# Repeated rows ordered by tokens, blend's softmax by channels, weights quantised on GpSimd, tokens in halves ahead of the indices

## The reference, cut to what matters

```
y = x @ weight[id[b]].T + bias[id[b]]           # cond, one weight per sequence
q, k = silu(y Wq), silu(y Wk); rotate by cos/sin(theta * token); v = y Wv
o = (tril(q k^T) v) Wo * sigmoid(y G1 G2); x = x + layernorm(o)
ctx = causal_ema(x, tau_ctx)
g   = x * sigmoid([x, ctx] Wg + bg)
mod = 0.5 + sigmoid(gelu(x Wn1) Wn2)            # 8 factors for each token
traces[d] = causal_ema(g * mod[d], tau[d])      # 8 of them
temporal = sum_d traces[d] * softmax(blend, axis=0)[d]    # blend is 8 x 256
z = layernorm((gelu(x Wsoma) * sigmoid(temporal Wtemp)) Wout)
x = x + ffn(z)     # bit-linear: weights to -1, 0, 1 by their mean |w|; activations to 8 bits
```

## Time and profile before

| | before |
|---|---|
| median of 3 runs | 710.37 us |
| the profiled execution, its own time | 707.44 us |
| its span in the profile | 705.5 us |
| TensorE busy | 642.1 us (91%) |
| VectorE busy | 549.7 us (78%) |
| ScalarE busy | 302.4 us (43%) |
| GpSimd busy | 309.2 us (44%) |
| share of the DMA B<-g_rows in the chain that ended last | 5% |

### The profile page before, as it was taken

The page is one execution under the profiler, slowest core; times in us unless marked ns, Lnnn a source line. Parts: engine busy times, 40 slices in busy tenths (PEclk is TensorE's granted clock), DMA queues, the critical chain, the costliest instruction groups (busy, mean ns, idle before and its releaser), DMA issues.

```text
span 705.5 us, 15004 instructions
## 1 busy us (share of the span) xinstructions
PE 642.1 (91%) x5766; PEld 472.1 (67%) x5766; DVE 549.7 (78%) x1068; ACT 302.4 (43%) x632; POOL 309.2 (44%) x313
## 2 busy tenths in 40 slices
PE   5689689999999999999999999999999999976653
PEld 3457467767777777778777777877786777764331
DVE  7789775878787778778797878787887978876864
ACT  4183334453544543534445444445344444533211
POOL 1260642435364726446362627272554626441222
PEclk9699899999999999999999999999999999999786
DMA  8411122215251634242341525152433325153322
...
DMA packets 77034, 53.36 MB, mean 76 GB/s; under 512 B 57251, under 2 KB 69795, under 8 KB 76323
## 3 DMA queue, kind: packets, MB, share of 16 engines
...
## 4 chain that ended last, share of the span: by engine, by line
PE 76%; DVE 10%; DMA 9%; issue 3%; POOL 1%; ACT 0%; POOLq 0%; SPq 0%; ACTq 0%; DVEq 0%
PE ps L475 69%; PE ps L478 7%; DMA B<-g_rows 5%; DMA g_rows<-G 2%; DVE B L905 2%; DVE EB L911 1%; DVE HP L908 1%; DMA HQ<-HM 1%; DVE EB L905 1%; DVE EB L908 1%; DVE FH L914 1%; DMA TT<-bpack 0%; DVE X L908 0%; DVE ZN L911 0%; DVE BN L1082 0%
## 5 line engine op out<-in xcount | busy, mean ns | idle before, releaser
L905 DVE TENSOR_TENSOR B<-B,BLGS 128x1024 f32<-128x1024 f32 x64 | 99.4, 1592 | 19.0 <-DMA B<-g_rows 18.8
L1207 POOL TENSOR_SCALAR HP<-HP,FT 128x1024 f32<-128x1024 f32 x32 | 41.2, 1289 | 149.2 <-DVE FT L908 149.2
L475 PE MATMUL ps<-WQ,YT 128*128 128x512 f32 (+1 forms) x256 | 88.1, 488 | 0.9 <-ACT YT L735 0.9
L905 DVE TENSOR_TENSOR EB<-ps,C 128x512 f32<-128x512 f32 x128 | 79.2, 680 | 8.2 <-PE ps L475 8.2
L475 PE MATMUL ps<-X1T,W 128*128 128x256 f32 x320 | 80.7, 383 | 1.5 <-DVE CT L1035 1.2
L905 DVE TENSOR_TENSOR HP<-FH,ps 128x512 f32<-128x512 f32 x64 | 42.4, 685 | 45.6 <-ACT FH L735 45.4
L475 PEld LDWEIGHTS ps<-WQ,YT 128*128 128x128 f32 x256 | 48.2, 190 | 36.1 <-issue 30.2
L475 PEld LDWEIGHTS ps<-X1T,W 128*128 128x128 f32 x320 | 58.3, 190 | 9.3 <-DVE CT L1035 2.0
L475 PE MATMUL ps<-FW,ZQ 128*128 128x512 bf16 x256 | 61.9, 386 | 0.0
L1160 POOL TENSOR_TENSOR X<-X,B 128x256 f32<-128x256 f32 x32 | 25.4, 797 | 67.6 <-DMA X<-x 67.6
L735 ACT ACT_TABLE_LOAD x40 | 51.3, 1283 | 2.3 <-PEq L1302 1.6
...
## 6 DMA issues: line engine op xcount, KB each, us to landing
...
W<-wpack SPq DMA_DIRECT2D x1, 1833.0 KB, 10.4
```

The lines of the kernel that those rows point to most:

```text
L475: return e0.matmul(o, l, r, start=start, stop=stop, skip_group_check=True)
L905: return e0.tensor_tensor(o, x, y, op)
L1207: e0.tensor_scalar(HP[:, s, :], HP[:, s, :], FT[:, s, 2:3], MAGIC, ALU.mult, ALU.add).then_inc(g["hx"], 1)
```

## The change

It does nine things, and reorders all five lists.

```diff
 gr (SP): rows repeated by token; MODT in one DMA; the constants follow
-... GS[s].rearrange("i q c -> i (q c)").unsqueeze(0).to_broadcast([4, 32, NJ * CH])
+... GS[s].rearrange("i q c -> i (q c)").unsqueeze(1).to_broadcast([32, 4, NJ * CH])
-                for r in range(4):
-                    e0.dma_start(MODT[32 * r:32 * r + 32, s, :]..., MS[s, :, :, :, r, :]...)
+                e0.dma_start(MODT[:, s, :]..., MS[s].rearrange("j q i r n -> (i r) (j q) n"))
-  "diff": np.maximum(f[:, :32] - p % 32, 0),  "low": (f[:, :32] >= p % 32) * 1.0
+  "diff": np.maximum(f[:, :32] - p // 4, 0),  "low": (f[:, :32] >= p // 4) * 1.0
 gr (SP) no longer waits for the blend weights, b4 does
-                e.wait_ge(a["blg"], 4)
-                e.wait_ge(d["ubl"], 16)
+                e.wait_ge(d["blg"], 16)          # in b4 (VectorE)
 blend: 16 numbers on each of 128 partitions, part of wpack
-            e0.dma_start(BL[:, :], bpack[BLEND].partition_broadcast(P))
+        BL = w_("blend").rearrange("p (d h) -> p h d", h=2)
+                red(MX[:, 0, :], BL, ALU.max)
+                tt(BL, BL, MX[:, 0, :]..., ALU.subtract)       # VectorE, in tab0
+                af(BL, BL, ACT.Exp)
+                red(MX[:, 1, :], BL, ALU.add)                  # VectorE, in tab2
+                e0.reciprocal(MX[:, 1, :], MX[:, 1, :])
+                tt(BL, BL, MX[:, 1, :]..., ALU.mult)
+                e0.dma_start(US.rearrange("d (h p) -> p (d h)", p=P), w_("blend"), ...)   # uw: pieces of 4 bytes
+            def blg(n):                                        # SP instead of ScalarE
+                e.wait_ge(d["uw"], 16)
+                e0.dma_start(BLGS[:, :], US....to_broadcast([32, 4, 2 * CH]))
 quant: VectorE keeps the scale (wsc: two small instructions), GpSimd has the three passes
+            def quant(n):                                      # GpSimd
+                e0.tensor_scalar(w, w, WS[:, 3 + n:4 + n], MAGIC, ALU.mult, ALU.add)
+                e0.tensor_scalar(w, w, MAGIC + 1, MAGIC - 1, ALU.min, ALU.max)
+                e0.tensor_scalar(FW[:, n, :], w, -MAGIC, 1.0, ALU.add, ALU.mult)
 HM: two buffers, each in the first half of its own HP
-        HM = sb("HM", [P, 1024], bf16)
+        HM = HP[:, :, :].bitcast(bf16)
-                e.wait_ge(d["hq0"], 16 * ((c + 1) // 2))       # hm (GpSimd)
-                e.wait_ge(d["hq1"], 16 * (c // 2))
+                e.wait_ge(d[f"hq{s}"], 16 * (c // 2))          # fs (VectorE)
 tokens: two halves with a semaphore each, the first ahead of the indices
             e0.dma_start(IDS[:, :], ids)
+            tokens(0, 0)
             load(0)
             e0.dma_start(WQ[:, :, :], wqkv)
+            tokens(0, 1)
 VectorE's first cast is gone
-            e0.tensor_copy(IDB[:, :], ident)
 orders, the parts that the prediction speaks of
-PE_HEAD  cond0 proj0 proj1 ktr0 qtr0 low0 ktr1 e0 qtr1 cond1 o0 gate0 e1 ... soma1 ema0
+PE_HEAD  cond0 proj0 cond1 proj1 ktr0 ktr1 qtr0 qtr1 e0 low0 e1 o0 low1 ... u0 ema0 soma1
-PE_PERIOD ... gtr(2k-2) wo proj gu gtr ttr dn o u low wo temp proj xtr ktr wout xtr wout qtr soma gate ema(2k-2) ...
+PE_PERIOD ... gtr(2k-2) temp gu o low gu gtr wsum wo wout wout ktr xtr qtr proj dn xtr gate u ema(2k-2) ...
-PE_TAIL  ... wg15 h1 ztr26 dn24 mod ztr27 gu26 ema29 gtr30 gu27 gtr31 ttr14 dn25 u temp14 wout28 wout29 ema30 ztr28 dn26 ztr29 gu28 ema31 ...
+PE_TAIL  ... dn24 ztr26 ztr27 dn25 gu26 gu27 xtr30 temp14 xtr31 soma14 h1 wg15 wout28 wout29 gtr30 gtr31 mod dn26 u soma15 ztr28 ztr29 gu28 gu29 ema30 ema31 ttr15 ...
-POOL_HEAD rk0 rk1 xb0 xb1 blend0 rs0 xb2 rs1 rk2 x1_0 x1_1 rk3 blend1 rk4 rs2 x1_2 ...
+POOL_HEAD rk0 rk1 rk2 xb0 xb1 rs0 rs1 x1_0 x1_1 rk3 quant0 xb2 xb3 quant1 rs2 rk4 x1_2 ...
-SP_TAIL  ... mw15 gw30 gr30 mr15 gw31 hq26 gr31 ...
+SP_TAIL  ... gw30 st gw31 mw15 gr30 mr15 gr31 ...
```

More of the change, by code:

```diff
@@ L26 @@
 BPS = BP["ga"][0]
-BLEND = slice(BPN, BPN + 2048)
 CP = {}
@@ L38 @@
 PE_HEAD = (
[L39 to L42, removed]
@@ L43 @@
[L43 to L44 removed]
+    ("cond", 0), ("proj", 0), ("cond", 1), ("proj", 1), ("ktr", 0), ("ktr", 1), ("qtr", 0), ("qtr", 1), ("e", 0), ("low", 0), ("e", 1),
+    ("o", 0), ("low", 1), ("proj", 2), ("gate", 0), ("o", 1), ("wo", 0), ("wo", 1), ("gate", 1), ("qtr", 2), ("wsum", 0), ("ktr", 2),
+    ("proj", 3), ("wsum", 1), ("xtr", 0), ("cond", 2), ("xtr", 1), ("qtr", 3), ("e", 2), ("h1", 0), ("wg", 0), ("o", 2), ("mod", 0),
@@ L45 @@
+    ("ktr", 3), ("gtr", 0), ("wo", 2), ("e", 3), ("proj", 4), ("o", 3), ("low", 2), ("gtr", 1), ("wo", 3), ("soma", 0), ("ktr", 4),
+    ("qtr", 4), ("xtr", 2), ("proj", 5), ("xtr", 3), ("gate", 2), ("u", 0), ("ema", 0), ("soma", 1), ("e", 4), ("h1", 1), ("wsum", 2),
+    ("wg", 1),
 )
 PE_PERIOD = (
-    ("ktr", 2, 1), ("qtr", 2, 1), ("cond", 1, 1), ("dn", 2, -8), ("mod", 1, -1), ("ztr", 2, -5), ("gu", 2, -6), ("o", 2, 0),
-    ("ema", 2, -3), ("e", 2, 1), ("gtr", 2, -2), ("wo", 2, 0), ("proj", 2, 2), ("gu", 2, -5), ("gtr", 2, -1), ("ttr", 1, -2),
@@ L49 @@
-    ("dn", 2, -7), ("o", 2, 1), ("u", 1, -1), ("low", 1, 1), ("wo", 2, 1), ("temp", 1, -2), ("proj", 2, 3), ("wsum", 1, 1),
-    ("xtr", 2, 0), ("ktr", 2, 2), ("wout", 2, -4), ("xtr", 2, 1), ("wout", 2, -3), ("qtr", 2, 2), ("soma", 1, 0), ("gate", 1, 1),
-    ("ema", 2, -2), ("e", 2, 2), ("wg", 1, 0), ("h1", 1, 0), ("ztr", 2, -4),
+    ("ktr", 2, 1), ("cond", 1, 1), ("qtr", 2, 1), ("ztr", 2, -5), ("mod", 1, -1), ("dn", 2, -8), ("o", 2, 0), ("ema", 2, -3),
+    ("proj", 2, 2), ("ttr", 1, -2), ("wo", 2, 0), ("e", 2, 1), ("gtr", 2, -2), ("temp", 1, -2), ("gu", 2, -6), ("o", 2, 1),
@@ L52 @@
+    ("low", 1, 1), ("gu", 2, -5), ("gtr", 2, -1), ("wsum", 1, 1), ("wo", 2, 1), ("wout", 2, -4), ("wout", 2, -3), ("ktr", 2, 2),
+    ("xtr", 2, 0), ("qtr", 2, 2), ("proj", 2, 3), ("dn", 2, -7), ("xtr", 2, 1), ("gate", 1, 1), ("u", 1, -1), ("ema", 2, -2),
+    ("soma", 1, 0), ("e", 2, 2), ("h1", 1, 0), ("wg", 1, 0), ("ztr", 2, -4),
 )
 PE_TAIL = (
-    ("ktr", 2, -5), ("qtr", 2, -5), ("cond", 1, -2), ("dn", 2, -14), ("mod", 1, -4), ("ztr", 2, -11), ("gu", 2, -12), ("o", 2, -6),
-    ("ema", 2, -9), ("e", 2, -5), ("gtr", 2, -8), ("wo", 2, -6), ("proj", 2, -4), ("gu", 2, -11), ("gtr", 2, -7), ("ttr", 1, -5),
@@ L56 @@
[L56 to L67, removed]
@@ L68 @@
-    ("temp", 1, -2), ("wout", 2, -4), ("wout", 2, -3), ("ema", 2, -2), ("ztr", 2, -4), ("dn", 2, -6), ("ztr", 2, -3), ("gu", 2, -4),
-    ("ema", 2, -1), ("gu", 2, -3), ("ttr", 1, -1), ("dn", 2, -5), ("temp", 1, -1), ("wout", 2, -2), ("wout", 2, -1), ("ztr", 2, -2),
-    ("dn", 2, -4), ("ztr", 2, -1), ("gu", 2, -2), ("gu", 2, -1), ("dn", 2, -3), ("dn", 2, -2), ("dn", 2, -1),
+    ("cond", 1, -2), ("qtr", 2, -5), ("mod", 1, -4), ("ktr", 2, -5), ("o", 2, -6), ("low", 1, -2), ("ema", 2, -9), ("dn", 2, -14),
@@ new lines @@
+    ("gtr", 2, -8), ("gtr", 2, -7), ("proj", 2, -4), ("e", 2, -5), ("ttr", 1, -5), ("wo", 2, -6), ("gu", 2, -12), ("proj", 2, -3),
+    ("temp", 1, -5), ("ztr", 2, -11), ("qtr", 2, -4), ("o", 2, -5), ("dn", 2, -13), ("wout", 2, -10), ("ktr", 2, -4), ("wout", 2, -9),
+    ("wo", 2, -5), ("gu", 2, -11), ("cond", 1, -1), ("gate", 1, -2), ("u", 1, -4), ("ema", 2, -8), ("qtr", 2, -3), ("ktr", 2, -3),
[3 rows of a table added]
+    ("gtr", 2, -6), ("mod", 1, -3), ("e", 2, -2), ("gtr", 2, -5), ("xtr", 2, -4), ("xtr", 2, -3), ("wout", 2, -8), ("wout", 2, -7),
@@ new lines @@
+    ("proj", 2, -1), ("gate", 1, -1), ("o", 2, -2), ("wg", 1, -2), ("h1", 1, -2), ("dn", 2, -10), ("ztr", 2, -8), ("dn", 2, -9),
+    ("ztr", 2, -7), ("mod", 1, -2), ("qtr", 2, -1), ("gu", 2, -8), ("u", 1, -3), ("ema", 2, -6), ("gu", 2, -7), ("gtr", 2, -4),
+    ("gtr", 2, -3), ("ktr", 2, -1), ("ema", 2, -5), ("u", 1, -2), ("ttr", 1, -3), ("e", 2, -1), ("temp", 1, -3), ("o", 2, -1),
+    ("wout", 2, -6), ("wout", 2, -5), ("ema", 2, -4), ("ema", 2, -3), ("wo", 2, -2), ("wo", 2, -1), ("ttr", 1, -2), ("dn", 2, -8),
@@ new lines @@
+    ("ztr", 2, -6), ("ztr", 2, -5), ("dn", 2, -7), ("gu", 2, -6), ("gu", 2, -5), ("xtr", 2, -2), ("temp", 1, -2), ("xtr", 2, -1),
+    ("soma", 1, -2), ("h1", 1, -1), ("wg", 1, -1), ("wout", 2, -4), ("wout", 2, -3), ("gtr", 2, -2), ("gtr", 2, -1), ("mod", 1, -1),
+    ("dn", 2, -6), ("u", 1, -1), ("soma", 1, -1), ("ztr", 2, -4), ("ztr", 2, -3), ("gu", 2, -4), ("gu", 2, -3), ("ema", 2, -2),
+    ("ema", 2, -1), ("ttr", 1, -1), ("dn", 2, -5), ("temp", 1, -1), ("wout", 2, -2), ("wout", 2, -1), ("dn", 2, -4), ("dn", 2, -3),
```

140 lines of the change are left out of this document (67 added, 73 removed), and 119 rows, old and new, of tables (ACT_HEAD, ACT_PERIOD, ACT_TAIL, DVE_PERIOD).

## The result

| | before | after |
|---|---|---|
| median of 4 runs | 710.25 us (708.60 to 710.71) | 682.92 us (682.02 to 688.13) |
| profiled execution: own time, span | 707.44, 705.5 us | 682.62, 680.8 us |
| its mean granted clock | 0.96 | 0.98 |

The ratio is 0.9635, with a 95% interval of 0.9592 to 0.9678: the kernel is faster by 27 us. The two profiled executions differ by 24.7 us in span.

The account below looks back on a forecast made before the run. TensorE's own list was taken to bound the middle, with losses in the two ends. Head 16, middle 0 and tail 12 make 28 us off 707.44: 679.4, plus 2.9 for the median 682.4, forecast 683, range 672 to 698.

Parts of the forecast that it names:

- The rows: Reading back the gated rows (gr): 16 DMA engines instead of 4, landing in 3.4 us instead of 8.80 to 9.78.
- The head, 16 us: Stretch up to the first ema and just behind it: 16 us saved (6 to 21), first ema at about 80 us.
- The quantisations, 7.9: Head: quant 0 and 1 leave VectorE's chain before the first ema, 7.9 us off that chain.
- The gr term (6.4): Head: the faster reading back of the gated rows takes 6.4 us off the chain before the first ema.
- TensorE's cap: Head: of 23.4 us off the chain, TensorE's own list before the first ema lets at most 22.8 be gained.
- The write of the blend row: Head, uw in 4-byte pieces: 8 us, bounds 3.7 and 30; costs 0, or 10 in the head at 30 us.
- The cold start, 4 us: Head: TensorE still waits for the rotation chain before 25 us and starts at a low clock; 4 us stay lost.
- The middle, 0: From 177 to 600 us TensorE's list stays the bound: no change, with an order effect of 2 us either way.
- The slack: Middle: 16.1 us of TensorE's list against 7.1 plus gr, so a landing up to 9.0 us makes no wait.
- The tail, 12 us: From gw 30 to the end: 12 us saved (7 to 16), faster rows and gr 31 right behind gr 30.
- GpSimd's quantisations: Rival: passes on GpSimd hold up the head, 7.7 us per quant; head gives 6 instead of 16; 694 us, chance 0.23.
- Rows that don't come faster: Rival: TensorE waits in each middle period, up to 1.5 us, and both ends lose savings; 713 us, chance 0.07.

Follow-up runs that it names:

- after_k8: The changed kernel with the source of gr written as 8 x 4 x 4 rows, to split it over 8 DMA engines; the landing did not change; 686.00 us.
- after_hm_single: The changed kernel with one HM buffer of its own again and the waits of before; 685.63 us.
- after_mr_four: The changed kernel, rows by tokens, with MODT read in four pieces of 8 tokens instead of one; 684.36 us.
- rows_in_before: The kernel before with only gr's rows read as 32 x 4, its constants, BLGS by DMA and MODT in one read, all orders as before; 699.61 us.

## Why the prediction was right, and where not

- *The rows.* Right: within a read the share is 0.82 in place of 0.25, 13 engines' worth instead of 4. The landing is 4.3 us (3.6 to 5.3) and not 3.4. The Trainium skill, page "DMA: Bandwidth & Descriptors", section "Why a DMA increments its semaphore by 16 and not by 1", gives the split by the slowest dimension: the traces agree for both forms (74 GB/s at 0.25, 270 at 0.82).
- *The head, 16 us.* 15.6 at gw 4, but the match is in part luck: the prediction left the low clock of the start in, and where it stayed in (after_k8, after_hm_single, after_mr_four) gw 4 came only 9.8 to 12.4 us earlier. The quantisations, 7.9, are 7.5 to 7.8 at gw 0 and 4 to 8 at the end. The gr term (6.4) is 1.9 alone, at gw 4, since GpSimd's rs, og and x1 are next; the prediction had this only as TensorE's cap. First ema at 77.53, where I had said about 80 (it comes at 83.35 in after_k8, with its slower start); TensorE idle for 10.6 us before 25, where I had said below 16.
- *The write of the blend row.* The mis-sized term. I took 8 us between bounds of 3.7 and 30; it takes 10.8 to 12.2. That it costs nothing hangs on its place, and "if it took 30 us, 10 in the head" missed that it holds the queue for the loads behind it, and that the order is part of the edit: late, it costs 12 us at 12 us.
- *The cold start, 4 us.* I let it stay. It differs from execution to execution, see below; in the profiled one most of it is gone (0.05 of 33.71 us lost between 25.10 and 62.00, where it was 0.17 of 33.31).
- *The middle, 0.* It gives back 2.5 us between gw 4 and gw 22, just over my bound of 2, and 3.9 up to gw 30. TensorE has gaps there, 3.3 us in 382.8, and gaps in the middle were what I had called a sign of being wrong; they are small, and their cause is open. The slack that I worked out from the earlier trace rows, a landing of up to 9.0 us, is too wide for rows in blocks: landings of 8.6 to 8.8 us already make TensorE wait, with a transpose and four MODT issues between gw and gr that I had not counted. A landing of 4.3 us makes no wait.
- *The tail, 12 us.* 13.0 from gw 30 to the end, 52.6 us (I had said under 52); gr 30 and gr 31 are 2.8 us apart, as predicted (within 3). 5.2 of it is the rows (in rows_in_before, with MODT in one read), and 7.8 the new lists. That gr 31 follows gr 30 at once can be 3.6 of these (6.4 - 2.8); the rest isn't taken apart.
- *The sum.* I had 28 off the profiled execution and it is 24.8; that the median of before stands 2.9 us above its profiled execution, which I added, doesn't hold for after (0.3). The two errors, 3.2 and 2.6, all but cancel in the forecast of 683; that it meets 682.92 so closely is luck.
- *The rivals.* GpSimd's quantisations did not take the place: they take 6.4 and 6.2 us, not 7.7, 3.2 us of VectorE's time lost beside them are seen in two instructions (1.9 and 1.3), and moving them back costs time. Rows that don't come faster: priced at 713, measured at 742.7. The period's loss of up to 1.5 was somewhat low (2.1), and missed were the four MODT issues within the ring, the slow read of the blend weights' copies in the head, the MOD writes behind the reads, and the 24 us of the last chunks.

Not shown: how the 19 us divide among the five lists. Only SP's first list was tried by itself, and going back to it costs 12 to 15 us.
